# LayerNorm of the next stage worked out inside the stage before it, in a twelve-stage fp32 network

## What is computed

```python
def _layernorm(x, axis=-1, eps=1e-05):
    m = jnp.mean(x, axis=axis, keepdims=True)
    v = jnp.var(x, axis=axis, keepdims=True)
    return (x - m) / jnp.sqrt(v + eps)
...
x = x + _L0_xattn_ref(_layernorm(x), ctx_768, ...)   # stage xattn0
x = x + _L0_attn_ref(_layernorm(x), ...)             # attn0
x = x + _L0_ffn_ref(_layernorm(x), ...)              # fp4_ffn
x = x + _L1_xattn_ref(_layernorm(x), ctx_768, ...)   # xattn1
x = x + _L1_attn_ref(_layernorm(x), ..., gamma)      # attn1
x = x + _L1_ffn_ref(_layernorm(x), W, b, V_r, C)     # low_rank
x = x + _L2_xattn_ref(_layernorm(x), ctx_768, ...)   # xattn2
x = x + _L2_attn_ref(_layernorm(x), ...)             # scan
x = x + _L2_ffn_ref(_layernorm(x), ...)              # moe_capacity
x = x + _L3_xattn_ref(_layernorm(x), ctx_768, ...)   # xattn3
x = x + _L3_attn_ref(_layernorm(x), ...)             # attn3
x = x + _L3_ffn_ref(_layernorm(x), ...)              # moe
```

## Time and profile before

| | us |
|---|---|
| median of 3 runs | 1914.64 (1912.82 to 1915.15) |
| the profiled execution | 1909.2 |
| its span, first to last instruction | 1907.0 |
| PE busy | 1602.8 |
| DVE busy | 1125.1 |
| ACT busy | 822.1 |
| POOL busy | 761.8 |
| mean granted TensorE clock | 0.911 of 2.4 GHz |

### The profile page before, as it was taken

How to read it: one execution, slowest core, us unless ns; L and a number is a source line. 1 busy time by engine, 2 the same in 40 slices (tenths; PEclk the granted TensorE clock), 3 DMA queues, 4 the chain that set the end, 5 groups by cost and what they waited for, 6 DMA issues and landing times. The chain is left out here.

```text
span 1907.0 us, 35283 instructions
## 1 busy us (share of the span) xinstructions
PE 1602.8 (84%) x12373; PEld 1358.6 (71%) x12373; DVE 1125.1 (59%) x3117; ACT 822.1 (43%) x2394; POOL 761.8 (40%) x927
## 2 busy tenths in 40 slices
PE   6999999666868999976999999699869477739996
PEld 6899889434547999846889998646569334528995
DVE  5887876488746888644767767459721322432222
ACT  4666666113326888712666666320123022113332
POOL 6666565352329999513211111147532111030111
PEclk9999999878979999987999999999879777859998
DMA  8545543200032333206233333160152573911112
GB/s 259 178 147 179 167 150 130 76 1 1 0 120 79 129 127 137 68 19 195 95 108 106 119 107 130 69 208 1 50 184 83 137 202 116 360 45 40 40 34 86
DMA packets 139710, 213.70 MB, mean 112 GB/s; under 512 B 19450, under 2 KB 106434, under 8 KB 139058
## 3 DMA queue, kind: packets, MB, share of 16 engines
q1 hardware_dynamic: 132418, 199.50, 32.5%
q0 software_dynamic: 3408, 8.54, 1.3%
q10 hardware_dynamic: 3712, 3.41, 0.6%
HBM read 170.07 MB, written 47.78 MB: 114 GB/s over the span
## 5 line engine op out<-in xcount | busy, mean ns | idle before, releaser
L802 DVE TENSOR_SCALAR xattn_oT<-bank,xattn_last 128x256 f32<-128x256 f32 x256 | 111.7, 478 | 90.7 <-PE bank L623 90.6
L708 ACT ACTIVATE xattn_probs<-bank,xattn_negmax 128x257 f32<-128x257 f32 x256 | 123.7, 483 | 65.6 <-DVE xattn_negmax L783 65.5
L713 ACT ACTIVATE xattn_probs<-xattn_probs,xattn_rsum 128x257 f32<-128x257 f32 x256 | 131.8, 515 | 1.4 <-DVE xattn_rsum L787 1.4
L1028 POOL TENSOR_SCALAR xattn_probs<-xattn_probs,xattn_rsum 128x257 f32<-128x257 f32 x128 | 119.5, 934 | 22.8 <-DVE xattn_rsum L1263 22.8
L783 DVE TENSOR_REDUCE xattn_negmax<-bank 128x1 f32<-128x257 f32 x256 | 106.4, 416 | 34.9 <-PE bank L596 33.4
L792 DVE TENSOR_TENSOR xattn_probsT_lo<-bank,xattn_probsT_hi 128x256 fp32r<-128x256 f32 x256 | 104.9, 410 | 9.8 <-ACT xattn_probsT_hi L719 8.7
L603 PE MATMUL bank<-ident,xattn_probs 128*128 128x128 f32 x512 | 103.9, 285 | 7.1 <-ACT xattn_probs L713 6.7
L719 ACT CAST xattn_probsT_hi<-bank 128x256 fp32r<-128x256 f32 x256 | 95.4, 373 | 32.3 <-PE bank L603 28.2
L541 POOL COPY ctx_stat<-xattn_mv 128x2 f32<-128x2 f32 x32 | 6.0, 187 | 237.7 <-DVE xattn_mv L816 237.7
L592 PE MATMUL bank<-xattn_ctxT,xattn_qk_hi 128*128 128x258 f32 x256 | 93.8, 366 | 0.5 <-DVE xattn_qk L779 0.5
L2121 POOL TENSOR_TENSOR scan_product<-scan_state,scan_qT 128x512 f32<-128x512 f32 x64 | 75.6, 1182 | 36.2 <-DVE scan_state L2258 35.8
(11 more groups left out here) (503 smaller groups left out, 5297.0 us busy)
## 6 DMA issues: line engine op xcount, KB each, us to landing
xattn_ctxT<-ctx_partsT SPq DMA_DIRECT2D x64, 516.0 KB, 3.9
xattn_ctxN<-ctx_partsN SPq DMA_DIRECT2D x64, 384.0 KB, 4.4
ctx_partsT<-xattn_ctxT SPq DMA_DIRECT2D x32, 516.0 KB, 2.7
moe_w<-in_L_ffn_W SPq DMA_DIRECT2D x16, 1024.0 KB, 13.7
ctx_partsN<-xattn_ctxN SPq DMA_DIRECT2D x32, 384.0 KB, 3.6
moecap_w_early<-in_L_ffn_w SPq DMA_DIRECT2D x10, 1024.0 KB, 13.1
xattn_rawN<-in_ctx SPq DMA_DIRECT2D x32, 192.0 KB, 2.7
xattn_raw<-in_ctx SPq DMA_DIRECT2D x32, 192.0 KB, 4.4
```

The costliest lines, as they stand in the source:

```text
L708: nc.scalar.activation(probs[:, n % RING, :], SB[n % 2][:, 0:KV], ACT.Exp, bias=negmax[:, n % RING:n % RING + 1], accum_out=psum[:, n % RI ...
L713: nc.scalar.mul(probs[:, n % RING, :], probs[:, n % RING, :], rsum[:, n % RING:n % RING + 1]).then_inc(norm_ready, 1)
L802: nc.vector.tensor_scalar(oT[k][:, heads, b, :], by_head(OB[:, k * 2 * P:(k + 1) * 2 * P]), last[:, k, j * PER_TILE + b:j * PER_TILE + b + ...
L1028: nc.gpsimd.tensor_scalar(probs[:, n % RING, :], probs[:, n % RING, :], rsum[:, n % RING:n % RING + 1], None, ALU.mult).then_inc(norm_read ...
```

## The change

Seven boundaries get it: xattn0 to attn0, fp4_ffn to xattn1, xattn1 to attn1, attn1 to low_rank, low_rank to xattn2, xattn2 to scan, and xattn3 to attn3. A new class `NextNorm` belongs to the earlier stage. As soon as a tile of `x` has its last value, DVE makes its moments (`bn_stats`, `bn_aggr`), POOL its factor (one column: plus eps, power), and DVE then writes that tile of `core.xn`. In the later stage `Norm(ahead=True)` leaves the DVE and POOL parts out and the waits for `xn` with them; the transposes and copies stay. The places of the three steps are written into each stage's loop by hand. In the wide attention they stand at fixed unit steps of the tile after next, in xattn1 at steps 12, 13 and 15 of the next tile, in attn1 and low_rank directly behind each write of `x` (with the `xn` of the tile before last), and in xattn3 at every second step, with four tiles' worth behind the loop. The start of xattn0 and four other boundaries keep the old form.

```diff
@@ -74 +74 @@
-    def __init__(self, st, twice=False, xn=None):
-        self.core, self.twice = st.core, twice
+    def __init__(self, st, twice=False, xn=None, ahead=False):
+
+        self.core, self.twice, self.ahead = st.core, twice, ahead
         self.xn = st.core.xn[:, :, :] if xn is None else xn
+        self.turned = st.sem("ln_turned")
+        self.xnT_ready = st.sem("ln_xnT_ready")
+        if ahead:
+            return
...
@@ -110 +122 @@
         nc = self.core.nc
+        if self.ahead:
+            return
...
@@ -125 +139 @@
         for t in range(TILES) if group is None else self.HALVES[group]:
-            pe.wait_ge(self.xn_ready, t + 1)
+            self.wait_xn(pe, t + 1)
...
@@ -142 +156 @@
+class NextNorm:
+
+
+    def __init__(self, st, x_done):
+        self.core, self.x_done = st.core, x_done
+        self.stats, self.mv = st.sb("next_stats", [P, TILES, 6]), st.sb("next_mv", [P, TILES, 2])
+        self.veps, self.rstd = st.sb("next_veps", [P, TILES]), st.sb("next_rstd", [P, TILES])
+        self.shift = st.sb("next_shift", [P, TILES])
+        self.stats_done, self.mv_ready = st.sem("next_stats_done"), st.sem("next_mv_ready")
+        self.veps_done, self.rstd_ready = st.sem("next_veps_done"), st.sem("next_rstd_ready")
+        self.shift_ready, self.xn_ready = st.sem("next_shift_ready"), st.sem("next_xn_ready")
+
+    def moments(self, dve, t, added):
+
+        nc = self.core.nc
+        dve.wait_ge(self.x_done, added)
+        nc.vector.bn_stats(self.stats[:, t, :], self.core.x[:, t, :]).then_inc(self.stats_done, 1)
+        dve.wait_ge(self.stats_done, t + 1)
+        nc.vector.bn_aggr(self.mv[:, t, :], self.stats[:, t, :]).then_inc(self.mv_ready, 1)
+
+    def factor(self, pool, t, shift=False):
+
+        nc, of = self.core.nc, slice(t, t + 1)
+        pool.wait_ge(self.mv_ready, t + 1)
+        nc.gpsimd.tensor_scalar(self.veps[:, of], self.mv[:, t, 1:2], EPS, None, ALU.add).then_inc(self.veps_done, 1)
+        pool.wait_ge(self.veps_done, t + 1)
+        nc.gpsimd.tensor_tensor(self.rstd[:, of], self.veps[:, of], self.core.neghalf[:, of], ALU.pow).then_inc(self.rstd_ready, 1)
+        if shift:
+            pool.wait_ge(self.rstd_ready, t + 1)
+            nc.gpsimd.tensor_tensor(self.shift[:, of], self.mv[:, t, 0:1], self.rstd[:, of], ALU.mult).then_inc(self.shift_ready, 1)
+
+    def normalise(self, dve, t):
+        dve.wait_ge(self.rstd_ready, t + 1)
+        self.core.nc.vector.tensor_scalar(self.core.xn[:, t, :], self.core.x[:, t, :], self.mv[:, t, 0:1], self.rstd[:, t:t + 1],
+                                          ALU.subtract, ALU.mult).then_inc(self.xn_ready, 1)
+
+
         st = Stage(core, ctx, "lowrank")
-        ln = Norm(st)
+        ln = Norm(st, ahead=True)
...
@@ -173 +225 @@
             pool.wait_ge(loaded, 16 * LOADS)
-            pool.wait_ge(ln.xn_ready, TILES)
+            ln.wait_xn(pool, TILES)
                 nc.gpsimd.tensor_tensor(core.x[:, t, :], core.x[:, t, :], b[:, :], ALU.add).then_inc(b_added, 1)
+            for t in range(TILES):
+                next_ln.factor(pool, t)
...
@@ -215 +269 @@
                                         ALU.add).then_inc(x_done, 1)
+                next_ln.moments(dve, t, t + 1)
+                if t >= 2:
+                    next_ln.normalise(dve, t - 2)
+            for t in (TILES - 2, TILES - 1):
+                next_ln.normalise(dve, t)
...
@@ -287 +346 @@
     M_FILLS, M_START = 1 + GROUPS, 3
+    FACTOR = 10 if first else 8
+    MOMENTS, NORMALISE = 2 * UNITS + 1, 2 * UNITS + 9
         st = Stage(core, ctx, name)
-        ln = Norm(st)
+        ln = Norm(st, ahead=not first)
...
@@ -518 +580 @@
             pool.wait_ge(bo_loaded, 16)
-            pool.wait_ge(ln.xn_ready, TILES)
+            ln.wait_xn(pool, TILES)
                 for n in range(UNITS - SPLIT, BATCH * PIECES):
+                    done, piece_of = divmod(n, PIECES)
+                    if piece_of == 0 and done >= FACTOR and (done - FACTOR) % PER_TILE == 0:
+                        next_ln.factor(pool, (done - FACTOR) // PER_TILE)
...
@@ -543 +608 @@
                         nc.gpsimd.tensor_tensor(cn.stat[:, 1 + k, :, n], veps[:, :, n], half[:, k, :], ALU.pow).then_inc(stat_ready, 1)
+                    if n >= FACTOR and (n - FACTOR) % PER_TILE == 0:
+                        next_ln.factor(pool, (n - FACTOR) // PER_TILE)
+            for t in range((BATCH - 1 - FACTOR) // PER_TILE + 1, TILES):
+                next_ln.factor(pool, t)
...
@@ -886 +955 @@
                     add(j - 1)
+                if t >= MOMENTS and (t - MOMENTS) % UNITS == 0:
+                    next_ln.moments(dve, (t - MOMENTS) // UNITS, (t - MOMENTS) // UNITS + 1)
+                if t >= NORMALISE and (t - NORMALISE) % UNITS == 0:
+                    next_ln.normalise(dve, (t - NORMALISE) // UNITS)
...
@@ -898 +971 @@
                         last_statistics()
+            next_ln.moments(dve, TILES - 1, TILES)
+            next_ln.normalise(dve, TILES - 1)
...
@@ -1049 +1125 @@
                         pool.wait_ge(bo_loaded, 16)
-                        pool.wait_ge(ln.xn_ready, TILES)
+                        ln.wait_xn(pool, TILES)
                     nc.gpsimd.tensor_tensor(core.x[:, t, :], core.x[:, t, :], bo_s[:, :], ALU.add).then_inc(bo_added, 1)
+                if 0 < j < TILES and s == ADD + 2:
+                    next_ln.factor(pool, j - 1)
+            next_ln.factor(pool, TILES - 1)
...
@@ -1291 +1370 @@
                     add(j - 1)
+                if j and s == ADD + 1:
+                    next_ln.moments(dve, j - 1, j)
+                if j and s == ADD + 4:
+                    next_ln.normalise(dve, j - 1)
...
@@ -1879 +1972 @@
                 quantise_h(t)
+                if t >= 2:
+                    next_ln.factor(pool, t - 2)
+            for t in (TILES - 2, TILES - 1):
+                next_ln.factor(pool, t)
...
@@ -2031 +2128 @@
                     add(s - 2)
+                    next_ln.moments(dve, s - 2, s - 1)
+                if s >= 3:
+                    next_ln.normalise(dve, s - 3)
+            next_ln.normalise(dve, TILES - 1)
...
@@ -3468 +3572 @@
                     add((s - 6) // 2)
+                if s >= 8 and s % 2 == 0:
+                    for t in (s - 8, s - 7):
+                        next_ln.moments(dve, t, (s - 8) // 2 + 1)
+                if s >= 10 and s % 2 == 0:
+                    for t in (s - 10, s - 9):
+                        next_ln.normalise(dve, t)
                     sums(s - 2)
+            for t in (TILES - 2, TILES - 1):
+                next_ln.moments(dve, t, TILES // 2)
+            for t in range(TILES - 4, TILES):
+                next_ln.normalise(dve, t)
```

30 lines of the change are left out of this document (21 added, 9 removed).

## The result

| | before | changed | ratio (95% interval) |
|---|---|---|---|
| median, 4 runs each | 1913.73 us | 1932.32 us (1926.96 to 1937.41) | 1.0103 (1.0067 to 1.0140) |
| span of the profiled execution | 1907.0 | 1924.8 | |
| mean granted clock | 0.911 | 0.914 | |

The account below looks back on a forecast made before the run. It took TensorE (PE, busy 84% of the span) as the limit, with chains at stage boundaries. Boundary and loop terms summed to +18.0 us on the profiled 1909.2, giving 1932.6 us on the 1914.64 median; range 1918 to 1947.

Parts of the forecast that it names:

- The price ahead of the barrier: Last tile's LayerNorm chain after the last write of x: 2.0 us per boundary, 2.5 at the upper end, paid seven times.
- What ends last behind the barrier: At each of seven boundaries, time is won only if LayerNorm, not something else such as a load, ended last.
- boundaries 4, 5 and 6: attn1 to low_rank, low_rank to xattn2, xattn2 to scan: nothing won behind the barrier; net +5.2, +4.4 and +2.0 us.
- boundary 2: fp4_ffn to xattn1: only the 1.41 us wait for xn to win; net +0.6, and +0.3 us for loop inserts.
- boundary 3: xattn1 to attn1: at most 2.9 us won before the last load lands, 2.6 taken; net −0.6 us.
- boundary 7: xattn3 to attn3: last xn done at +4.65 us, gain 0.45 behind the barrier; net +4.2 us.
- The DVE-paced loops: attn1 and low_rank: x writes 1.03 and 1.37 us apart in attn1, 0.97 and 1.30 in low_rank, lengthening both loops.
- Boundary 1's gain: xattn0 to attn0: bias ends at +14.4 instead of +18.5 us, 3.5 of 4.1 counted as gain; net −1.5.
- The loops: Inserts inside xattn0, xattn1 and xattn2: 3.0 us taken for all three stages, ends 0 and 18.
- xattn3: Tail with four xn behind the last addition, net +4.2 us, and moments ahead of softmax sums in the loop, +0.45.
- The port rival: Shared DVE and POOL port holds xn: xattn1 1.5 us a tile, xattn0 1.0; +32.5 us, 1947; chance 0.13.

Follow-up runs that it names:

- experiment 3: Changed kernel with xattn1's three inserts moved from steps 12, 13 and 15 of the next tile to 5, 9 and 11 of the tile after next: ratio 1.0098.
- experiment 2: Changed kernel with attn1 to low_rank and low_rank to xattn2 put back to the old form, the other five boundaries as changed: ratio 1.0054.
- experiment 1: Kernel before with the new form only from xattn0 to attn0, the old form at the other six boundaries: ratio 0.9983.
- experiments 3 and 4: experiment 3 has its own line; the other is the changed kernel with only POOL's xattn1 factor moved, to step 9 of the tile after next: 1931.69 us.
- experiment 8: Changed kernel with the eighth tile's LayerNorm done at the start of the next stage at all seven boundaries, attn0's clearings behind it: ratio 1.0063.

## Why the prediction was right, and where it was not

- **The price ahead of the barrier** was right: 2.0 us forecast, and from the end of the last write to the end of its xn 2.09 to 2.18 measured at the six boundaries with one tile per write, in every kernel with the whole new form there. One case is longer: 2.30 at the end of xattn1 in experiment 3, where two tiles' factors stood behind the loop. It was worked out from single rows and the hand-overs between engines, and the one unseen duration (the power over one column) was 0.57 by the nearest row's 0.55.
- **What ends last behind the barrier** was right at boundaries 4, 5 and 6: the offsets of the first gated instruction moved by 0.1, −0.7 and +0.3 us when LayerNorm went away, and experiment 2 put LayerNorm back behind boundaries 4 and 5 with at most a few tenths lost. At boundary 2 the start gave 1.8 where 1.4 was forecast: xattn1's first addition came 75.9 us after the start and 77.7 before. At boundary 3 the first projection moved from +7.7 to +4.9, a gain of 2.8 where 2.6 was taken. At boundary 7 it moved from +7.7 to +7.5, for which 0.45 was taken; in the other kernels with the new form it came at +6.4 to +7.3, each time behind the same load.
- **The DVE-paced loops** of attn1 and low_rank were right: pitches of 1.04 and 1.37 (forecast 1.03 and 1.37), 1.00 and 1.31 (0.97 and 1.30), and +3.9 for low_rank where +4.4 was forecast, with its first addition 0.8 us earlier, which is in the scatter described in experiment 2.
- **Boundary 1's gain** was sized a little too low: 3.5 forecast, while DVE's first copy comes 3.9 earlier, and attn0 with fp4_ffn is 3.9 shorter in experiment 1, where boundary 2 has no tail. In the changed kernel they are 4.5 shorter although they carry boundary 2's tail of 2.1; but four other kernels with the same code there had 193.4 to 193.9 us instead of 191.2, so more than 2 of that is scatter. What the copy doesn't explain lies behind it in attn0 (last section), where the forecast had no term. The step that took too much off is "I count 3.5 of the 4.1, since PE's projections then fall more into the stretch in which it has just been idle".
- **The loops** were sized too low: "I take 3.0 for all three stages". xattn1 alone lost 0.6 us on each of five tiles and 0.5 on each of the other two, 3.9 us (the last one by comparison at a clock of 1.00: 18.5 and 18.0); xattn0 lost 1.4. xattn2 lost none up to its sixth addition (302.5 us after the start and 302.6 before) and 0.5 from there to the seventh, 32.2 and 31.7, as xattn0 did; no experiment tells why at that place. That makes some 5.7 in all, within the 0 to 8 that the forecast's own range allowed. The text named the reason, that by totals the time is free and not by place, but looked for it in POOL and the port. In xattn1 it was DVE's own order (experiments 3 and 4). The rows to read would have been DVE's timeline at the steps of the inserts, not its idle sum over a window.
- **xattn3** shows +1.3 where +5.1 was forecast, and this is the clock. The windows of the kernel before ahead of its second addition:

```profile
1560.00:1574.00 14.00, 14.00 (x69) 7.61 (x66) 3.07 (x10) 3.75 (x9) 0.32 (x2) 0.50 0.47 127
1574.00:1592.00 18.00, 15.76 (x97) 8.03 (x99) 3.41 (x12) 3.86 (x9) 0.32 (x2) 0.62 0.27 75
```

and of the changed kernel in the same part of the stage:

```profile
1572.00:1584.00 12.00, 11.84 (x106) 6.39 (x105) 3.85 (x12) 3.75 (x9) 0.39 (x3) 0.83 0.62 166
1584.00:1600.00 16.00, 10.05 (x78) 5.75 (x82) 2.84 (x11) 3.86 (x9) 0.26 (x2) 0.79 0.40 99
```

From the second addition to the third, before and in the change:

```profile
1591.92:1601.40 9.48, 7.43 (x69) 4.38 (x69) 1.34 (x5) 3.46 (x8) 0.00 (x0) 1.00 0.01 2
1599.70:1613.82 14.12, 11.69 (x69) 6.43 (x69) 2.25 (x9) 3.46 (x8) 1.60 (x4) 0.64 0.01 1
```

PE ran in the first two windows with a granted clock of 0.50 (1.2 GHz) and 0.62 before and 0.83 and 0.79 in the change, and the first addition of x came 7.3 us earlier in the stage, before any instruction of the change had run there. From the second addition to the third it had 0.64 where the kernel before had 1.00, which gave 4.6 us back. The stage took from 93.0 to 107.2 us in four kernels that left it alone. The terms themselves were right: the tail grew by 4.3, and in experiment 8, at a clock of 1.00, the inserts lengthened this last stretch from 9.5 to 9.9 us, 0.4 where 0.45 was forecast. One thing stays open: in five of the six kernels with the inserts this stretch ran at 0.62 to 0.64 and took 13.8 to 14.1 us, while without them it ran at 1.00 in three kernels and at 0.81 in the fourth (11.5 us). Whether the inserts bring the lower clock about was not tested; the forecast had no term for it. So the agreement of 17.8 with 18.0 in one pair of profiles is closer than the theory deserves. By the table, xattn0 and xattn1 were 3.6 above their forecasts and the stages without an edit 3.4, while attn0 with fp4_ffn lay 3.3 and xattn3 3.8 below.
- **The port rival** did not come about: its 1.5 and 1.0 us a tile were never seen. In xattn1 six of seven xn in the loop ran beside POOL's instructions at their own 0.41 (the seventh took 0.48), and POOL's next one took 1.02 instead of 0.93:

```profile
717.26 0.62 POOL L1100 TENSOR_TENSOR xattn_q_blocks<-xattn_q_lo,xattn_own 128x256 fp32r<-128x256 f32 x1
...
717.86 1.02 POOL L1104 TENSOR_SCALAR xattn_probs<-xattn_probs,xattn_rsum 128x257 f32<-128x257 f32 x1
...
717.68 0.41 DVE L192 TENSOR_SCALAR xn<-x,xattn_next_mv,xattn_next_rstd 128x256 f32<-128x256 f32 x1
```

In fp4_ffn it did happen, five times: the xn ends 0.14 us after POOL's instruction does, and takes 0.91.

```profile
502.94 1.52 POOL L1905 TENSOR_TENSOR fp_fp_q<-fp_fp_q,fp_h_sign 128x704 bf16<-128x704 bf16 x1 [3.56 <-DVE fp_fp_q L1898]
...
503.69 0.91 DVE L192 TENSOR_SCALAR xn<-x,fp_next_mv,fp_next_rstd 128x256 f32<-128x256 f32 x1
```

It cost nothing there, since PE paces that loop (additions 8.33 us apart in both kernels). In experiment 3 it happened in xattn1 too, for 0.2 us a tile. And in the kernel before it was one xn of the four that was held in attn0: it ran from 358.58 to 365.61, 0.15 us past the end of the second clearing, and the other three took 0.4 each. The Trainium skill ("SBUF — State Buffer", Who interferes with whom) has the lock as exclusive for a whole instruction of whichever engine came first. The fp4_ffn rows agree with that, and so do the 7.99 us in attn0 as far as the xn had to wait, though it stood behind two instructions of POOL that followed each other without a gap, not one; the xn in xattn1 that began at 717.68, inside POOL's instruction of 717.26 to 717.88, doesn't show it. Why, no run here tells.

## What to carry to other kernels

Moving work ahead of a barrier doesn't hide it for the last item: its chain over the engines (here 2.1 us, made of 1.0 us of DVE's work, 0.8 of POOL's and the hand-overs between them) moves onto the path in full, and what it buys is only what isn't hidden behind loads on the other side. So look first at what ends the first wait behind the barrier, boundary by boundary; five of seven were loads. And when an insert is to be free, look for gaps at its own steps in the engine's timeline, since idle time summed over a window says nothing of where it lies.
